# Row ranges of 46 instead of 64 nodes, and 11 of 1564 gathers moved from GpSimd to single-row copies on SyncE, in a graph layer on one core

## What is computed

```python
edge_index_t = jnp.stack([src, dst], axis=1)
nodes = node_state[edges].reshape(num_edges, -1)            # x[src], x[dst]
gates = ssp(edge_state @ We1 + be1) @ We2 + be2
gates = gates * (1.0 - sigmoid(5.0 * (edges_distance - 3.5)))
h = ssp(nodes @ Wn1 + bn1) @ Wn2 + bn2
message_sum = zeros_like(node_state).at[edges[:, 1]].add(h * gates)
new_state = node_state + (ssp(message_sum @ Ws1 + bs1) @ Ws2 + bs2)
x = layernorm(x + new_state)                                 # ssp(v) = softplus(v) - log 2
```

## Time and profile before

| what | value |
|---|---|
| median of 3 runs | 1993.46 us (1991.19 to 1993.7) |
| profiled execution | span 1988.8 us; its page gives no other time of its own, so what lies around the span is taken as the difference to the median, 4.7 us |
| TensorE busy | 1737.7 us, 87% of the span |
| ScalarE busy | 1532.1 us, 77% |
| GpSimd busy | 1484.7 us, 75% |
| VectorE busy | 1285.6 us, 65% |
| DMA | 157.78 MB, mean 79 GB/s |

### The profile page before, as it was taken

One profiled execution on the slowest core, in us unless ns is written; L12 is line 12 of the kernel. 1 busy time (PEld: TensorE's weight loads), 2 busy tenths in 40 slices (PEclk: granted clock), 3 DMA queues, 4 the chain that ended last, 5 costly groups with the idle time before them and its releaser, 6 DMA issues.

```text
span 1988.8 us, 53540 instructions
## 1 busy us (share of the span) xinstructions
PE 1737.7 (87%) x16249; PEld 1328.7 (67%) x16249; DVE 1285.6 (65%) x3512; ACT 1532.1 (77%) x3368; POOL 1484.7 (75%) x1572
## 2 busy tenths in 40 slices
PE   4699999898888988878889988998988898988987
PEld 3577777676666666666666766766666676766666
DVE  4578888666665655555656666666666666666666
ACT  3589999777777777777777788788777787787877
POOL 7777777777777777777777777777777777777773
PEclk7799999999999899999989999899999899999999
DMA  5433333333333333333333333333333233333331
GB/s 122 122 85 98 97 97 97 85 85 76 91 74 73 71 73 70 75 68 71 74 71 74 74 80 74 74 75 78 74 75 75 69 84 75 75 78 75 75 76 38
DMA packets 256432, 157.78 MB, mean 79 GB/s; under 512 B 45401, under 2 KB 227046, under 8 KB 256366
## 3 DMA queue, kind: packets, MB, share of 16 engines
q1 hardware_dynamic: 202652, 104.94, 18.2%
q0 software_dynamic: 50048, 51.35, 15.5%
q10 hardware_dynamic: 3666, 0.68, 0.2%
HBM read 146.94 MB, written 9.87 MB: 79 GB/s over the span
## 4 chain that ended last, share of the span: by engine, by line
POOL 57%; issue 22%; PE 11%; DVE 3%; ACT 2%; SPq 2%; DMA 2%; DVEq 1%; ACTq 1%; POOLq 0%
POOL ga L459 57%; PE ps L623 3%; PE ps L636 3%; PE ps L640 1%; DVE hid L1113 1%; SPq L340 1%; PE ps L585 1%; DMA ga<-in_x_dram,srcT 1%; PE ps L575 1%; DVE hid L1117 1%; PE ps L653 1%; PE ps L662 1%; PE ps L577 0%; DVEq L1139 0%; ACT lg L861 0%
## 5 line engine op out<-in xcount | busy, mean ns | idle before, releaser
L459 POOL DMA_INDIRECT ga<-in_x_dram,srcT x1564 | 1483.7, 949 | 477.6 <-issue 472.4
L852 ACT ACTIVATE lg<-ps,bn1c 128x512 f32<-128x512 f32 x391 | 268.4, 687 | 306.6 <-PE ps L585 267.6
L636 PE MATMUL ps<-wn,hid 128*128 128x64 f32 x3128 | 447.9, 288 | 18.9 <-DVE hid L1117 17.1
L1113 DVE SCALAR_TENSOR_TENSOR hid<-ps,neg_b,lg 128x512 f32<-128x512 f32 x391 | 292.8, 749 | 221.9 <-ACT lg L867 205.2
L636 PEld LDWEIGHTS ps<-wn,hid 128*128 128x128 f32 x3128 | 393.1, 197 | 51.5 <-DVE hid L1117 26.6
L575 PE MATMUL ps<-ident,ea 128*128 128x128 f32 x782 | 173.8, 305 | 198.2 <-DMA ga<-in_x_dram,srcT 135.2
L844 ACT COPY xe<-ps 128x512 f32<-128x512 f32 x391 | 229.9, 588 | 113.3 <-PE ps L577 99.8
L623 PE MATMUL ps<-xe,wn 64*128 64x256 f32 x1564 | 289.8, 449 | 0.0
L1151 DVE TENSOR_TENSOR acc<-acc,ps 64x64 f32 x782 | 168.4, 215 | 163.7 <-issue 157.9
L640 PE MATMUL ps<-we,hid 128*128 128x128 f32 x1564 | 273.1, 299 | 0.0
L575 PEld LDWEIGHTS ps<-ident,ea 128*128 128x128 f32 x782 | 80.0, 143 | 282.1 <-issue 268.8
(11 more groups left out here) (124 smaller groups left out, 1847.9 us busy)
## 6 DMA issues: line engine op xcount, KB each, us to landing
ea<-in_edge_attr_dram SPq DMA_DIRECT2D x195, 256.0 KB
ga<-in_x_dram,srcT POOLq DMA_INDIRECT x1564
bw<-b_tab SPq DMA_DIRECT2D x782, 32.0 KB
relb<-rel_tab SPq DMA_DIRECT2D x196, 64.0 KB
b_tab<-share SPq DMA_DIRECT2D x25, 250.0 KB
out_dram<-xs SPq DMA_DIRECT2D x25, 125.0 KB
xs<-in_x_dram SPq DMA_DIRECT2D x3, 750.0 KB
rows_i<-in_dst_dram SPq DMA_DIRECT2D x1, 768.0 KB
```

The costliest lines, as they stand in the source:

```text
L459: pool.indirect_dma_start(to[:, t % 2, t // 2, :], None, x, bass.IndirectOffsetOnAxis(ap=idx[:, t:t + 1], axis=0)).then_inc(done, 16)
L636: pe.matmul(hg[:, t * D:(t + 1) * D], hid[:, u % 2, t * P:(t + 1) * P], wn2[:, :], start=False, stop=False, skip_group_check=True)
L852: act.activation(lg[:, u % 2, 0:QUAD].rearrange("p (k e) -> p k e", k=2), z[:, :, 0:PAIR], ACT.Abs, bias=bn1c[:, 0:1]).then_inc(n_abs, 1)
L1113: dve.scalar_tensor_tensor(out=hid[:, u % 2, 0:QUAD].rearrange("p (k e) -> p k e", k=2), in0=ps[:, 2 * (u % 2):2 * (u % 2) + 2, 0:PAIR], s ...
```

## The change

1. `W` goes from 64 to 46, everywhere: ranges copied into `bw` have 46 rows (they start at partition 0 and 64 as before, `HALF`), `oh` has 46 columns per row group, `flush` adds 46. In the inputs no pair's last node lies more than 36 behind its first, and 45 in the last range, whose first node is held at N - W, so the kernel stays on the same branch.
2. SyncE's places in `b_tab` come ready as byte offsets from a second table, `wb_all`, so the register arithmetic ahead of each `bw` copy goes. The table takes one more VectorE instruction, one more store and one more load on ScalarE's queue ahead of the loop, and `w_loaded` is now waited for at 32.
3. In eleven quads (48, 80, 112, ... 368) GpSimd issues three gathers, not four. The rows of the fourth group come by SyncE: 128 copies of one row (256 bytes) into `stage`, eight per turn over 16 turns, which begin 38 quads ahead (turns 10 to 40 for quad 48), the next quad's right behind, up to quad 361. Their addresses are loaded into registers eight at a time from `row_at`. In the turn four quads ahead of its quad SyncE copies `stage` to `ga` (`hand_rows`, 128 rows), and GpSimd's third gather of that quad waits for it (semaphore `handed`).
4. SyncE fetches the 1408 indices into `row_at` ahead of its loop, after waiting until ScalarE has evacuated all index rows (`row_e`), and VectorE multiplies them by 256 at the end of its step 7 (`row_ready`), for which SyncE waits in turn 10.
5. SyncE's loops are written out in full.

```diff
-W = 64
+HALF = 64
+W = 46
+ROWS0 = 48
+ROWS_EVERY = 32
+ROWS_N = 11
+ROWS_BEFORE = 38
+ROWS_TURN = (8,) * 16
...
                 for n, first in enumerate(firsts):
-                    sp.dma_start(bw[n % 2 * W:(n % 2 + 1) * W, v + n // 2, :],
-                                 b_tab[bass.ds(first, W), :]).then_inc(s_bw[v], 16)
+                    sp.dma_start(bw[n % 2 * HALF:n % 2 * HALF + W, v + n // 2, :].bitcast(U8),
+                                 b_bytes[bass.ds(first, W * F * 4)].rearrange("(r b) -> r b", b=F * 4)).then_inc(s_bw[v], 16)
+
+            def load_rows(q):
+
+                i, turn = divmod(q - (ROWS0 - ROWS_BEFORE), ROWS_EVERY)
+                turn //= 2
+                if not (q >= ROWS0 - ROWS_BEFORE and i < ROWS_N):
+                    return
+                if i == 0 and turn == 0:
+                    sp.wait_ge(row_ready, 1)
+                if i >= 2 and turn == 0:
+                    sp.wait_ge(xe_t, ROW_QUADS[i - 2] + 1)
+                first, n = ROWS_FIRST[turn], ROWS_TURN[turn]
+                _, places = nc.values_load_multi_w_load_instructions(
+                    row_at[:, i * P + first:i * P + first + n], engines=(mybir.EngineType.SP,), min_val=0,
...
+                for r, place in enumerate(places):
+                    sp.dma_start(stage[first + r:first + r + 1, i % 2, :].bitcast(U8),
+                                 x_bytes[bass.ds(place, D * 4)].rearrange("(r b) -> r b", r=1)).then_inc(s_stage[i % 2], 16)
+
+            def hand_rows(q):
+
+                i = (q - (ROWS0 - 4)) // ROWS_EVERY
+                if (q - (ROWS0 - 4)) % ROWS_EVERY or not 0 <= i < ROWS_N:
+                    return
+                quad = ROW_QUADS[i]
+                sp.wait_ge(s_stage[i % 2], P * 16 * (i // 2 + 1))
+                sp.wait_ge(xe_t, quad - (ARING - 1))
+                sp.dma_start(ga[:, quad % ARING, 1, 1, :], stage[:, i % 2, :]).then_inc(handed, 16)
...
                 load_rel(q, u)
                 load_bw(q, v, firsts)
                 if reached(q, RING):
                     load_ea(q, u)
+                load_rows(q)
+                hand_rows(q)
...
-                gather_rows(ga[:, q % ARING], srcT[:, 4 * q:4 * q + 4], s_ga[q % ARING])
+                to, idx, done = ga[:, q % ARING], srcT[:, 4 * q:4 * q + 4], s_ga[q % ARING]
+                if q in ROW_QUADS:
+
+                    gather(to, idx, 0, done)
+                    gather(to, idx, 1, done)
+                    pool.wait_ge(handed, 16 * (ROW_QUADS.index(q) + 1))
+                    gather(to, idx, 2, done, 32)
+                else:
+                    gather_rows(to, idx, done)
...
                 four_steps(1, 1, 0, False, True)
+                dve.wait_ge(ld_row, 16)
+                dve.tensor_scalar(row_at, row_at, float(D * 4), None, ALU.mult).then_inc(row_ready, 1)
```

More of the change, by code:

```diff
@@ L25 @@
 BRING = 8
+ROWS0 = 48
[3 more added lines that the diff above has]
+ROWS_TURN = (8,) * 16
+ROWS_FIRST = tuple(sum(ROWS_TURN[:n]) for n in range(len(ROWS_TURN)))
 IN_RANGE = "windows' places are the least of N - W and of destinations, which are nodes"
+IN_X = "sources are nodes"
 def reached(i, n):
@@ L85, in gnn_layer @@
     assert RG > 1 and RL > 1
+    ROW_QUADS = [ROWS0 + ROWS_EVERY * i for i in range(ROWS_N)]
+    assert sum(ROWS_TURN) == P and all(n % 4 == 0 for n in ROWS_TURN) and 2 * len(ROWS_TURN) == ROWS_EVERY
+    assert ROWS0 % 2 == 0 and ROWS0 >= ROWS_EVERY and ROW_QUADS[-1] < NQ - 4
     STEPS = 8
@@ L260, in gnn_layer @@
         g_oh, g_mm, g_add = ([sem(f"{n}{k}") for k in range(2)] for n in ("g_oh", "g_mm", "g_add"))
+        ld_row, row_ready, wb_ready, wb_stored = (sem(n) for n in ("ld_row", "row_ready", "wb_ready", "wb_stored"))
+        handed = sem("handed")
+        s_stage = [sem(f"s_stage{k}") for k in range(2)]
         filled, hg_set = sem("filled"), sem("hg_set")
@@ L378, in fast_step @@
                 _, firsts = nc.values_load_multi_w_load_instructions(
-                    w_all[0:1, bass.ds(q * 2, 2 * n)], engines=(mybir.EngineType.SP,), min_val=0, max_val=N - W,
+                    wb_all[0:1, bass.ds(q * 2, 2 * n)], engines=(mybir.EngineType.SP,), min_val=0, max_val=(N - W) * F * 4,
                     skip_runtime_bounds_check_because=IN_RANGE)
@@ L410, in _ @@
             with sp.Else():
+                sp.wait_ge(row_e, XCOLS)
+                sp.dma_start(row_at.rearrange("p (i e) -> p i e", e=P),
+                             src[(ROWS0 + 1 - ROWS_EVERY) * QUAD:(ROW_QUADS[-1] + 1) * QUAD].rearrange(
+                                 "(a i e) -> a i e", a=1, e=ROWS_EVERY * QUAD)[:, :, (ROWS_EVERY - 1) * QUAD + PAIR + 1:ROWS_EVERY * QUAD:2]).then_inc(ld_row, 16)
                 for q in range(BRING):
@@ L414, in _ @@
                     load_x(n)
-                for q in range(BRING, 2 * BRING):
-                    fast_step(q, q % BRING)
[L419 to L441, removed]
+                ahead = NODE0 + STEPS
+                for q in range(BRING, NQ):
+                    stored, made, node = (q - 12) // 4, (q - 7) // 4, (q - (ahead + STEPS - 1)) // STEPS
+                    if q % 4 == 0 and 1 <= stored < NG:
+                        share_stored(stored // 2, stored % 2)
+                    fast_step(q, q % BRING)
+                    if q % 4 == 3 and SHARES <= made < NG:
+                        store_share(made, made % 2)
+                    if q % STEPS == (ahead - 1) % STEPS and 0 <= node < EARLY:
+                        store(node)
             for g in range(EARLY, NG):
@@ L454, in _, with gather @@
             pool.iota(iota_pi[:, :], pattern=[[1, 1]], base=0, channel_multiplier=1).then_inc(iotas, 1)
+            def gather(to, idx, t, done, inc=16):
+                pool.indirect_dma_start(to[:, t % 2, t // 2, :], None, x,
+                                        bass.IndirectOffsetOnAxis(ap=idx[:, t:t + 1], axis=0)).then_inc(done, inc)
             def gather_rows(to, idx, done):
                 for t in range(4):
-                    pool.indirect_dma_start(to[:, t % 2, t // 2, :], None, x,
-                                            bass.IndirectOffsetOnAxis(ap=idx[:, t:t + 1], axis=0)).then_inc(done, 16)
+                    gather(to, idx, t, done)
             def fast_step(q):
@@ L621, in front @@
                         half = slice(k * D, (k + 1) * D)
-                        weights, rows = (wn1[half, 0, :], xe[half, u, 1, :]) if end == 0 else (bw[half, b, :], ohT[half, u % 2, :])
+                        near = slice(k * HALF, k * HALF + W)
+                        weights, rows = (wn1[half, 0, :], xe[half, u, 1, :]) if end == 0 else (bw[near, b, :], ohT[near, u % 2, :])
                         pe.matmul(ps[:, 2 * (u % 2) + k, 0:PAIR], weights, rows,
```

22 lines of the change are left out of this document (18 added, 4 removed).

## The result

| what | kernel before | changed kernel |
|---|---|---|
| median, same chip | 1992.33 us (4 runs, 1990.35 to 1993.7) | 2010.74 us (4 runs, 2005.46 to 2015.23) |
| ratio | | 1.009, 95% interval 1.0073 to 1.0106 |
| profiled execution | 1988.8 us of span | 2007.07 us, 2005.3 us of it span |

The change makes the kernel 0.9% slower. 1985.0 us were forecast, with a range to 2002; the time lies outside it.

The account below looks back on a forecast made before the run. The prediction took GpSimd's gathers to set the pace: 1993.46 us, less 13.75 for eleven gathers, plus a 5.3 us wait at the first hand-over, gives 1985.0 us. The range was 1979.5 to 2002 us.

Parts of the forecast that it names:

- What is taken away: GpSimd's gathers: eleven fewer at 1.25 us each save 13.75 us; the smaller ranges were taken as 0.
- The parts of SyncE's turn: SyncE's turn for two quads: `bw` 1.8, load of eight 1.2, eight one-row copies 2.9 us, plus smaller parts.
- The sum of the turn: SyncE's turn takes 8.0 us, bounds 6.9 and 11.1, fitting GpSimd's 10.0 and, barely, TensorE's 8.5.
- The shift ahead of turn 10: Preamble and first turns: extra store, load, index fetch and queued `bw` copies cost 2.0 us, bounds 0 and 4.
- TensorE's delay: At quad 12, `ea` issued later puts TensorE back by 4 to 5 us; 5 was taken.
- Where turn 44 begins: SyncE's turn that hands over quad 48's rows: 244 us by TensorE's pace, 241.6 by SyncE's own; 244 taken.
- The chain of the hand-over: From turn 44's begin until quad 48's rows land: 9.75 us, rows at 253.8, so GpSimd waits 5.3 us.
- The rival "slower": SyncE becomes the bound: break-even at a turn of about 8.6 us, slower by 0.2% from 8.9 on; chance 0.21.
- the rival that cancels: Gain and wait about cancel: turn 8.6 us, wait 13.5, 1993 us; or `bw` held up by `xs` loads, 1992; chance 0.19.

Follow-up runs that it names:

- the first set: On a chip where the kernel before takes 2537.95 us: W = 46 without rows 1.0181; with rows, W = 64, W = 48, or first quad 80: 1.1849, 1.1838, 1.1828.

## Why the prediction was wrong

Step by step, as the prediction has them:

- **What is taken away** was right: 1553 gathers, 13.75 us, as the account of the last gather above shows. `oh` went from 0.418 to 0.344 us and gave nothing back at the end; there 2.5 us were lost instead, beside a lower granted clock (0.888 for the run, 0.949 before).
- **The parts of SyncE's turn** were right or too dear, unstalled: one row 0.228 us (0.239 taken), load of eight 0.716 (1.2 taken, the lower half of its bounds), `bw` 0.254 (0.33 taken). The Trainium skill ("Runtime: NRT & Kernel Launch", section on instruction fetch mechanics) has about 200 ns for each register, and in its terms such a load is one from HBM, while these values lie in SBUF. No such rate shows here: on SyncE eight cost 0.24 us more than one, and VectorE, whose eight in 1.844 seemed to match, loads six in 0.84 at the end of the kernel before.
- **The sum of the turn** is the step that failed: 8.0 us forecast, 9.3 measured, with 6.7 to 7.0 if nothing stalls. It has no term for stalls, and 2.3 us a turn are waiting: 1.9 inside DMA issues, 0.4 for semaphores. The parts that were taken too dear hid about 1 us of it; without that luck the miss would be larger. The prediction weighed 46 rows on two DMA engines and set this aside ("far less than the two turns by which `bw` is early"): it asked only whether `bw` comes in time. What it left out is that other transfers get slower with it (`ea`, the gathers) and that SyncE itself stands at the next issue. The rule of the Trainium skill ("DMA: Bandwidth & Descriptors", section on why a DMA increments its semaphore by 16) was right: the packet counts agree with 2 engines for 46 rows, 16 for 48 and 64, 11 for 44 and 1 for 47.
- **The shift ahead of turn 10** was mis-sized, too: 2.0 us taken, bounds 0 and 4, and 7.6 measured. With W = 48 it is 0.8 (step 7 ends at 106.55), so this is the 46 rows again. In turn 8, behind the loads of `xs`, the issues of `bw` take 6.28 us (4.47 with W = 48), and the issues of those loads themselves 21.8 (19.4). W = 46 without row copies is late as well (turn 12 at 109.3, for 102.8 before and 100.0 with W = 48 and no rows).
- **TensorE's delay** was taken as 5 us: quad 12 transposed at 120.2. It was at 127.83, 12.6 us late, since the `ea` issued at 120.40 took 6.90 us to land. With W = 48 it was at 117.93.
- **Where turn 44 begins**: 244 forecast, 266.7 measured. By SyncE's own path the forecast had 241.6; of the 25.1 us between, turn 12 gives 4.6 (118.2 for 113.6) and sixteen turns of 9.28 instead of 8.0 the other 20.5. W = 48 with the same rows has turn 12 at 111.4, turns of 8.24 and its turn 44 at 243.2, within a microsecond of the forecast, and a wait of 2.9 us.
- **The chain of the hand-over** was right as a sum, 9.75 us forecast and 10.0 measured, partly by luck: in turn 44 `bw` took 2.5 us for 1.8 and the load of eight 0.7 for 1.2. That no later hand-over is waited for was right.
- **The rival "slower"** named what happened, and its table was good: at a turn of 9.3 it gives turn 44 at 263.3, a wait of 26 and 2006 us. It got a chance of 0.21, because its only way to a longer turn was a dear one-row issue; the stalls belonged there, and they were filed, at 7.4 us once, under the rival that cancels.
- What is argued rather than shown is where the stall is: that a full queue of the two engines holds up SyncE's issue. The traces count packets by queue and not by DMA engine, so the load of the two isn't seen. That fewer engines bring the stalls, and more end them, is shown.

The width by itself buys nothing (48 without rows: 0.9997). 46 without rows is at 1.0022, with an interval from 1.0002: at most a small loss, just clear of none. The gathers saved are worth 0.5 to 0.6% once the rows are on time; W = 48 with rows from quad 80 is the best of all, 1977.78 us, 0.9936 (0.9918 to 0.9955).

## What to carry to other kernels

Before shrinking a transfer, work out over how many DMA engines its rows divide, and charge what follows to every transfer that is under way at the same time and to the queue that issues it, not only to the transfer's reader. When a helper takes over part of the bounding engine's work, compare when the two meet: an engine that runs ahead by its full buffer meets a helper that is still catching up, and here it was cheaper to start the help 32 quads later, with ten gathers saved for eleven, than to be waited for once. A turn that barely fits deserves its own range: price it unstalled, then ask what one microsecond more in each turn does by the first meeting.

## What was not expected of the hardware

- The unstalled issue of a copy costs SyncE more with more engines, and on 16 engines more with more rows: `bw` 0.254 us on 2 engines (46 rows), 0.30 on 11 (44 rows), 0.37 on 16 with 48 rows and 0.54 with 64 (medians). With 46 rows the issues are cheaper than all of these and the turn is the longest but that of 47 rows, whose issues stall throughout.
- Narrower ranges go with a lower granted clock of TensorE. Two stretches of the kernel before and of that with W = 48 (us, busy of PE, PEld, DVE, ACT and POOL, clock, DMA share, GB/s); the first is the same for both, the second is not:

```profile
130.00:245.00 115.00, 113.53 (x1158) 89.50 (x1159) 92.46 (x252) 103.84 (x233) 86.96 (x93) 1.00 0.39 98
300.00:600.00 300.00, 267.81 (x2576) 207.09 (x2573) 207.16 (x556) 234.77 (x513) 227.14 (x240) 0.95 0.35 84
```

```profile
130.00:245.00 115.00, 113.71 (x1161) 89.68 (x1159) 90.26 (x253) 104.67 (x234) 87.01 (x92) 1.00 0.39 94
300.00:600.00 300.00, 284.69 (x2607) 221.02 (x2607) 203.69 (x563) 236.50 (x520) 226.98 (x240) 0.89 0.35 82
```

  A mean of 1.00 is the upper level, 2.4 GHz; 0.95 and 0.89 are mixtures with 1.2 GHz. In the second, TensorE is busy 16.9 us longer for nearly the same number of matmuls, and has the room for it. With W = 64 and rows the run has 0.943, with 48 0.907, and with 48 and no rows 0.898, so it goes with the width and not with the row copies. Why is open.
- The same program took 2537.95 us on one chip and 1992 on the others, and there the kernels of the first set lost 2 to 18%, where the same files gained 0.2 to 0.5% or lost 0.2% on others. A hand-over with a fixed lead is tuned to one ratio of the engines' speeds.
